# A block's products issued between the two octs of a step instead of behind both, in a two-layer relational graph network on one core

## The reference

```python
def _rgcn_layer(x, src, dst, edge_type, w_rel, root, bias):
    N = x.shape[0]
    seg = dst * NUM_REL + edge_type
    xs = x[src]
    sums = jax.ops.segment_sum(xs, seg, num_segments=N * NUM_REL)
    cnt = jax.ops.segment_sum(jnp.ones(seg.shape, x.dtype), seg, num_segments=N * NUM_REL)
    mean = (sums / jnp.maximum(cnt, 1.0)[:, None]).reshape(N, NUM_REL, -1)
    return jnp.einsum('nrd,rdo->no', mean, w_rel) + x @ root + bias
...
h = jax.nn.relu(_rgcn_layer(x, src, dst, edge_type, w_rel1, root1, b1))
return _rgcn_layer(h, src, dst, edge_type, w_rel2, root2, b2)
...
x = _layernorm(x + _L0_gnn_ref(...), axis=-1)
```

## Time and profile before

| what | value |
|---|---|
| median of three runs | 3990.43 us (3989.36 to 3991.66) |
| the profiled execution: as a run, its span | 3991.19 us, 3989.5 us |
| POOL busy | 2964.9 us (74%), 3140 instructions |
| TensorE busy (matmuls) | 2110.6 us (53%), 12375 |
| DVE busy | 2284.4 us (57%), 5258 |
| ACT busy | 942.0 us (24%), 3133 |
| mean granted TensorE clock | 0.753 of full |

### The profile page before, as it was taken

The page is one execution under the profiler, slowest core; times in us unless marked ns, Lnnn a source line. Parts: engine busy times, 40 slices in busy tenths (PEclk is TensorE's granted clock), DMA queues, the critical chain, the costliest instruction groups (busy, mean ns, idle before and its releaser), DMA issues. The chain is left out here.

```text
span 3989.5 us, 55805 instructions
## 1 busy us (share of the span) xinstructions
PE 2110.6 (53%) x12375; PEld 1980.0 (50%) x12376; DVE 2284.4 (57%) x5258; ACT 942.0 (24%) x3133; POOL 2964.9 (74%) x3140
## 2 busy tenths in 40 slices
PE   2655555555555555555535555555555555555554
PEld 2555555555555555555534454444444444444444
DVE  7866666666666666666624444444444444444444
ACT  1222222222222222222212222222222222222223
POOL 7777777777777777777567777777777777777775
PEclk9777777777777777777767777777777777777777
DMA  5322222222222222222122222222222222222221
GB/s 115 81 78 77 77 77 77 77 77 77 77 77 77 77 77 76 77 77 65 47 54 63 63 62 62 62 62 62 62 62 62 62 62 62 62 62 62 62 62 46
DMA packets 206601, 275.40 MB, mean 69 GB/s; under 512 B 62732, under 2 KB 156428, under 8 KB 206444
## 3 DMA queue, kind: packets, MB, share of 16 engines
q0 software_dynamic: 100032, 205.07, 19.9%
q1 hardware_dynamic: 101534, 67.96, 6.0%
q10 hardware_dynamic: 4878, 0.86, 0.2%
HBM read 260.85 MB, written 12.80 MB: 69 GB/s over the span
## 5 line engine op out<-in xcount | busy, mean ns | idle before, releaser
L1307 POOL DMA_INDIRECT rows<-table,idx_s x1563 | 1475.3, 944 | 507.4 <-issue 474.4
L1307 POOL DMA_INDIRECT rows<-in_x_dram,idx_s x1507 | 1424.7, 945 | 459.1 <-issue 455.8
L1607 PE MATMUL ps_agg<-S,rows 128*128 128x140 f32 x6272 | 1344.0, 381 | 0.0
L1607 PEld LDWEIGHTS ps_agg<-S,rows 128*128 128x128 f32 x6272 | 1315.6, 281 | 30.7 <-issue 0.2
L1865 DVE TENSOR_TENSOR ring<-ps_agg,ring 128x440 f32 x784 | 482.8, 616 | 1061.7 <-PE ps_agg L1607 1019.2
L1603 PE MATMUL ps_agg<-zero_b 128*128 128x440 bf16 x784 | 382.5, 488 | 937.3 <-DMA rows<-table,idx_s 792.0
L1603 PEld LDWEIGHTS ps_agg<-zero_b 128*128 128x128 bf16 x784 | 103.7, 132 | 991.0 <-issue 974.1
L1468 ACT COPY idx_s<-idx_t 128x8 uint32 (+1 forms) x385 | 83.4, 218 | 2112.7 <-PE ps_agg L1607 2112.1
L1901 DVE TENSOR_REDUCE z_s<-prod 128x128 f32<-128x1536 f32 (+1 forms) x196 | 563.0, 2872 | 5.5 <-ACT prod L1511 5.5
L1836 DVE TENSOR_TENSOR cnt_ring<-ps_agg,cnt_ring 10x14 f32 x1568 | 264.9, 169 | 517.7 <-PE ps_agg L1607 359.1
L1626 PE MATMUL ps_y<-wall,ring 128*128 128x128 f32 x3920 | 528.8, 288 | 12.9 <-ACT prod L1506 12.9
(11 more groups left out here) (119 smaller groups left out, 934.2 us busy)
## 6 DMA issues: line engine op xcount, KB each, us to landing
attr<-in_edge_attr_dram SPq DMA_DIRECT2D x97, 336.0 KB, 3.3
rows<-table,idx_s POOLq DMA_INDIRECT x1563
rows<-in_x_dram,idx_s POOLq DMA_INDIRECT x1507
x_in<-in_x_dram SPq DMA_DIRECT2D x97, 64.0 KB, 2.0
table<-h_s SPq DMA_DIRECT2D x97, 64.0 KB
x_in<-table SPq DMA_DIRECT2D x97, 64.0 KB, 1.8
prod<-in_x_dram SPq DMA_DIRECT2D x97, 64.0 KB
out_dram<-o_s SPq DMA_DIRECT2D x97, 64.0 KB
```

The costliest lines, as they stand in the source:

```text
L1307: pool.indirect_dma_start(out=rows[:, slot, j, :], out_offset=None, in_=(x, htab)[l][:, :], in_offset=bass.IndirectOffsetOnAxis(ap=at, axi ...
L1607: ins = t_.matmul(bank[:, bass.ds(off[j] * R, TCOL)], lhsT=rows[:, o % PER, j, :], rhs=S[:, o % PER, j, :], start=False, stop=(c == 3))
```

## The change

In each step the call of `transform` for block s-2 moves from behind the second `aggregate` to between the two. The waits inside it, the operands and the number of instructions are the same, and no other engine's program changes.

```diff
                             aggregate(l, i, 2 * k, off, last, ((k - 2) % PER, s * 4 - 2) if behind else None)
+                            if behind:
+                                transform(l, s - 2, (k - 2) % PER, s * 4 - 2,
+                                          (i if k > 0 else i - 1) * 16 + (l * LAPS * 16 + 16))
                             off = offsets(i * (2 * PER) + 2 * k + 1)
                             types = (s + 2, (k + 2) % PER) if l == 0 and not (last and k >= PER - 2) else None
                             aggregate(l, i, 2 * k + 1, off, last, typ=types)
-                            if behind:
-                                transform(l, s - 2, (k - 2) % PER, s * 4 - 2,
-                                          (i if k > 0 else i - 1) * 16 + (l * LAPS * 16 + 16))
```

## The result

The changed kernel took 3997.59 us (median of 19 runs, 3995.95 to 3999.10) against 3990.93 us for the kernel before (19 runs beside them, 3989.36 to 3992.59). Timed once more beside other kernels the changed one was 6.0 ± 1.0 us slower, so the change costs some 6.4 us. The forecast was 3.45 us, 3993.9 us, and its range ended at 3997.2. By the bound of 0.2% this is "within 0.2%", as forecast, but the size is not. The time lies only 0.4 us outside the range, and the kernel before took 0.5 us more in its 19 runs than in the three that the forecast stands on; what is well outside is the difference, 6.7 us against a sum of 3.45 us with bounds of 2.6 and 4.9.

What follows compares the result with a forecast made beforehand. POOL's issue of gathers, one each 1.25 us, was taken to bound the kernel. Inside the layers 0, plus 0.89 us and 2.56 us at the layer ends, 3.45 us on 3990.43, gave 3993.9 us; range 3991.0 to 3997.2.

Steps and rivals of the forecast that it cites:

- The change, inside the layers: nothing: Inside layers, the moved 2.57 us of products fit TensorE's 5.59 us wait for the odd oct's rows: no cost.
- bank waits: Inside layers, TensorE's waits for ACT to free a bank, costed at nothing; rival: they hold POOL, 4180 us, 1 in 100.
- the wait for rows grows from 3.0 us to 5.6 us, which costs nothing: In the step's other half, TensorE's wait for rows lengthens from 3.0 to 5.6 us, at no cost.
- The end of layer 0: Products ahead of the last oct's halves delay DVE, so layer 1 starts 0.89 us later; bounds 0.7 to 1.6 us.
- DVE's cover: At layer 0's end DVE runs behind TensorE and so hides 1.68 of the products' 2.57 us.
- The end of layer 1: DVE waits for TensorE there, so the products' whole 2.56 us delays the end; bounds 1.9 to 3.3 us.
- No cost: Rival: rows or DVE's own work hide the moved products at both layer ends, 3990.4 us; 10 in 100.
- The slow clock: Rival: moved products run wholly at 1.2 GHz, costing 8.8 us over both layer ends, 3999.2 us; 5 in 100.
- A gain: Rival: ACT waits for block 95's products, so earlier ones save up to 2.56 us per layer end, 3985.3 us; 2 in 100.

Runs made afterwards that it cites:

- after: The changed kernel, transform between the two octs in every step, against the kernel before: 3997.59 us, ratio 1.0018.
- g_after: The changed kernel timed again beside other kernels, against the kernel before: ratio 1.0016, +6.0 ± 1.0 us.
- g_after_tail: The changed kernel, with DVE's and ACT's block work ahead of the last oct's in each layer's last step, against the kernel before: ratio 0.9995, -2.6 ± 0.9 us.
- e2: Kernel before with transform moved between the octs in all steps but each layer's last, against the kernel before: ratio 1.0008, +3.3 ± 0.7 us.
- e1: Kernel before with transform moved between the octs only in each layer's last step, against the kernel before: ratio 1.0005, +2.3 ± 1.0 us.
- v1_tail: Kernel before; only in each layer's last step, transform between octs and DVE's and ACT's block work ahead of the last oct's: 3985.92 us, ratio 0.9985.
- e7: Kernel before plus four DVE additions of two SBUF tiles in each middle step of layer 1, against the kernel before: ratio 1.0102, +41.1 ± 3.4 us.
- e8: Kernel before plus four DVE additions, one input in PSUM, in each middle step of layer 1, against the kernel before: ratio 1.0001, +0.4 ± 0.8 us.
- e3: Kernel before plus 20 small zero products between the octs in all but each layer's last step, against the kernel before: ratio 1.0004, +1.6 ± 0.7 us.
- the small fold: Ring fold cut from 44 columns to 1, against the kernel before: changed kernel ratios 1.0013 and 1.0011, kernel before 0.9997.
- e5: Kernel before plus four DVE clearings of SBUF tiles in each middle step of layer 1, against the kernel before: ratio 1.0004, +1.8 ± 0.9 us.
- e6: Kernel before plus four DVE copies from PSUM in each middle step of layer 1, against the kernel before: ratio 0.9998, -0.2 ± 0.7 us.

## Why the prediction was wrong

1. **"The change, inside the layers: nothing"** is the step that failed. It checked that POOL waits for no one longer, and that was right: no wait for indices, and the odd oct's rows still come last where they did. For TensorE it was not quite right, which cost POOL no wait: the bank waits, costed at nothing, do appear early in layer 0 (3.8, 5.2 and 5.5 us ahead of the products at 128.21, 144.35 and 160.73, before 0.6 us once), and the even oct is held last by DVE's `hit_typ` or `S` in 38 + 17 steps of the two layers, before in 3 + 6. It said of the other half of the step that "the wait for rows grows from 3.0 us to 5.6 us, which costs nothing". With that pause every even oct of layer 1 is slow, and more than half of the odd ones are fast; DVE's first addition of the odd oct moves by 0.8 to 0.9 us against POOL's grid of gathers, and on average more of DVE's SBUF operations run over gathers' starts (59 to 83 gathers of over 0.96 us in after, g_after, g_after_tail and e2, 45 to 60 in before, e1 and v1_tail). Measured: e2 gives +3.3 ± 0.7 us with the last steps left alone; less some 0.3 us of the gap (32.40 against 32.1 on average), 3 us. g_after_tail against v1_tail gives 1.3 us less the ends, and 6.4 - 4.4 = 2.0 us is what is left of the whole. So 1.3 to 3 us, about 2. That such operations lengthen gathers is shown by e7 and e8. That this is the whole of the 2 us, and how they divide over the operations, is not: the excess agrees in size (2.7 us more), but the run that was to reproduce it without the group, e3, did not bring about the fast odd octs, and the small fold did not take the loss away. So the cause of the inside part stays partly open.
2. **The end of layer 0** was put at 0.89 us with bounds of 0.7 and 1.6. In after's own profile it was 0.78, in four profiles 2.0 on average, above the upper bound. The term took the even oct's second half at 1.27 us. With the longer pause ahead of that oct, the half took 2.07 us in three of the four, and the products began slow (2.08 to 2.40 us for the first 16 entries in place of 1.95). The working of DVE's cover (1.68 us hidden) held for after: the sums of the last oct's first half end 2.48 us later behind the last gather's start (1981.57 - 1974.76 against 1977.22 - 1972.89), DVE's start on them 0.82 us later.
3. **The end of layer 1** was put at 2.56 us and was 2.5 in after's profile, 2.4 on average. The products took 1.95 us between the octs, the plane sum's distance from the last gather grew from 6.25 to 8.81 us, ACT's taking of block 95 did not move ahead. Right in mechanism and size.
4. **The rivals.** "No cost" fell. "The slow clock" gave 8.8 us for both ends; its condition, a clock that rises later than the even oct's end plus 5 us, was never met. At the end of layer 0 the even oct did stay slow to its end in three profiles of four, but the products sped up within the group: 2.08 to 2.40 us for the first 16 entries, not the 3.75 us of the earlier trace rows. It had the right direction for layer 0 and did not hold for layer 1. "A gain" fell here, and so did "bank waits", whose waits came but never reached POOL; the gain of an earlier group is real only where the chain of TensorE, DVE and ACT sets the pace, as on the slower chip.

The sum as it should have been: 2.0 + 2.4 + about 2 = 6.4 us, the last being what the first two leave of the measured whole. The forecast had the first at 0.9 and the third at 0. The first error comes from an overlooked fact, that the group takes the short pause away from the even oct; that the third does too fits the excess but is not shown. That the end of layer 0 came out so near its forecast in after's own profile, 0.78 against 0.89 us, was luck: against the same 32.39 us of before the other three profiles have 1.9 to 2.1 us.

## What to carry to other kernels

Where the pacing engine issues gathers back to back, an order change on another engine is not free just because nobody waits: ask which operations it moves against the gathers' starts, and whether those have all their inputs in SBUF. When work moves from one idle stretch to another, the stretches change length, and with them which part of TensorE's work runs at the low clock; price the work behind a lengthened pause at both clocks, at the ends above all. The same edit can be worth -4.4% or +0.2% according to which chain sets the pace. And where one profile of each kernel suggests a cause of 1 or 2 us, look whether other profiles of the old order show it too: the fold seemed to be such a cause until those of e1_last_step_only and v1_tail were counted.

## What the runs showed of the hardware

- A DVE addition of 128x440 with both inputs in SBUF that runs over the start of an indirect gather holds it: up to 0.45 us for the 0.61 us folds (e1_last_step_only), and 39.5 us of excess in layer 1 with 336 added ones (e7), of which 158 ran over a start. With one input in PSUM: 0.4 ± 0.8 us (e8). A clearing of the same tile (e5) and a copy from PSUM (e6) hold nothing.
- In layer 1 the oct behind the long pause (6.3 to 6.4 us, medians) was slow in its first half in 97 or 98 of 98 steps (before, after), the oct behind the short one (2.9 us) was fast in 53 to 62 in the kernels without added work in layer 1. Where a granted clock was read for a slow half, in g_after, it was 0.50.
- One chip ran the same program 28% slower than the others (5097.5 against some 3991 us), at a granted clock of 0.66 of full against 0.75.
